# A part of the value product and the sum over keys moved in among the score tiles, in three attention cores on one Trainium2 core

## The reference

```python
x = x + jnp.tanh(g_xattn[n]) * xattn_ref(_layernorm(x), ctx_512, ...)
x = x + jnp.tanh(g_ffn[n]) * ffn_ref(_layernorm(x), ...)
```

```python
scores = jnp.einsum('bhsr,bhlr->bhsl', q_r, k_r)      # 16 heads, 56 queries, 1500 keys
attn = jax.nn.softmax(scores, axis=-1)
ctx_c = jnp.einsum('bhsl,bld->bhsd', attn, kv_rope)    # 64 wide
```

## Time and profile before

| | us |
|---|---|
| median of 3 runs | 2179.44 (2172.59 to 2183.32) |
| profiled execution | 2182.55 |
| its span, first to last instruction | 2180.8 |
| PE busy | 2052.8 |
| DVE busy | 1477.5 |
| POOL busy | 1356.4 |
| ACT busy | 1082.2 |

### The profile page before, as it was taken

The page is one execution under the profiler, slowest core; times in us unless marked ns, Lnnn a source line. Parts: engine busy times, 40 slices in busy tenths (PEclk is TensorE's granted clock), DMA queues, the critical chain, the costliest instruction groups (busy, mean ns, idle before and its releaser), DMA issues.

```text
span 2180.8 us, 34757 instructions
## 1 busy us (share of the span) xinstructions
PE 2052.8 (94%) x13336; PEld 1413.8 (65%) x13336; DVE 1477.5 (68%) x2141; ACT 1082.2 (50%) x1770; POOL 1356.4 (62%) x850
## 2 busy tenths in 40 slices
PE   7898999999999988899999999989998999999998
PEld 5586777755555556666555555488897555555588
DVE  6766872577887856766787887653335778878553
ACT  4452332565665645311566566444434656656543
POOL 0366883188788774455678778725441887887644
PEclk9898999999999998999999999999999999999999
DMA  3035877323223204101322322025533232232012
GB/s 97 3 118 162 249 230 211 93 57 80 63 57 81 48 30 129 34 1 35 84 57 65 78 58 66 7 87 156 146 95 76 58 80 63 58 80 49 32 46 76
DMA packets 65702, 179.56 MB, mean 82 GB/s; under 512 B 11280, under 2 KB 21280, under 8 KB 65154
## 3 DMA queue, kind: packets, MB, share of 16 engines
q1 hardware_dynamic: 65154, 177.01, 30.7%
q10 hardware_dynamic: 384, 0.33, 0.1%
HBM read 162.32 MB, written 14.98 MB: 81 GB/s over the span
## 4 chain that ended last, share of the span: by engine, by line
PE 76%; DVE 9%; ACT 4%; POOL 4%; issue 4%; DMA 1%; SPq 1%; POOLq 0%; DVEq 0%; ACTq 0%
PE psum L1529 19%; PE psum L946 19%; PE psum L1515 18%; PE psum L1405 5%; PE psum L1416 3%; ACT E L1984 3%; PE psum L1687 2%; PE psum L1546 2%; PE psum L1644 1%; DVE mx L2531 1%; PE psum L960 1%; POOL CL L2003 1%; PE psum L1339 1%; PE psum L1217 1%; PE psum L1237 1%
## 5 line engine op out<-in xcount | busy, mean ns | idle before, releaser
L2264 POOL TENSOR_TENSOR SA<-SA,E 125x896 f32<-125x896 f32 x288 | 605.9, 2104 | 19.1
L2531 DVE TENSOR_REDUCE mx<-psum 128x2 f32<-128x1000 f32 (+1 forms) x540 | 548.7, 1065 | 97.5 <-PE psum L1405 61.6
L1984 ACT ACTIVATE E<-psum 125x896 f32<-125x896 f32 x576 | 519.2, 920 | 128.4 <-PE psum L1515 101.2
L1529 PE MATMUL psum<-E,V 125*64 125x448 f32 x2304 | 459.5, 541 | 0.0
L1529 PEld LDWEIGHTS psum<-E,V 125*64 125x64 f32 x2304 | 159.9, 137 | 239.9 <-issue 228.1
L1515 PE MATMUL psum<-QH,KH 64*125 64x448 f32 x1152 | 256.1, 410 | 9.7 <-ACT E L1984 3.6
L2553 DVE RECIPROCAL RS<-psum 128x448 f32<-128x448 f32 x48 | 142.0, 2958 | 150.5 <-PE psum L1546 150.5
L1515 PE MATMUL psum<-QL,KH 64*125 64x448 f32 x1152 | 238.2, 363 | 0.0
L1515 PE MATMUL psum<-QH,KL 64*125 64x448 f32 x1152 | 222.4, 363 | 0.0
L1405 PE MATMUL psum<-KH,QH 64*128 64x500 f32 x864 | 194.9, 409 | 1.8 <-ACT QR L1926 1.6
L2264 POOL TENSOR_TENSOR SA<-SA,SB 125x896 f32<-125x896 f32 x45 | 105.7, 2348 | 132.8 <-DVE SB L2549 132.5
(11 more groups left out here) (310 smaller groups left out, 4179.5 us busy)
## 6 DMA issues: line engine op xcount, KB each, us to landing
KH<-kt_scratch SPq DMA_DIRECT2D x96, 375.0 KB, 5.2
KL<-kt_scratch SPq DMA_DIRECT2D x96, 375.0 KB, 6.8
EW<-in_f_w SPq DMA_DIRECT2D x64, 256.0 KB, 7.3
kt_scratch<-kt SPq DMA_DIRECT2D x16, 750.0 KB, 6.1
WS<-in_f_w SPq DMA_DIRECT2D x31, 384.0 KB, 4.9
GB<-gates_scratch SPq DMA_DIRECT2D x36, 224.0 KB, 3.9
slot_of_t<-slots_scratch SPq DMA_DIRECT2D x64, 112.0 KB, 3.8
WoT<-in_a_WoT SPq DMA_DIRECT2D x24, 256.0 KB, 3.4
```

The costliest lines, as they stand in the source:

```text
L1529: i = e.matmul(psum[c * DC:(c + 1) * DC, 4, 0:HT], V[0:LP, b, tile * DC:(tile + 1) * DC], E[g[n, b, k] % NE][0:LP, half[c]], start=k == 0, ...
L1984: e.activation(E[m % NE][0:LP, :].rearrange("p (c q) -> p c q", c=2), psum[0:LP, pair:pair + 2, 0:HT], ACT.Exp).then_inc(exp_set.sem, 1)
L2264: e.tensor_tensor(SA[b % 2][0:LP, :], a[0:LP, :], x[0:LP, :], ALU.add).then_inc(sum_set.sem, 1)
L2531: e.tensor_reduce(o, psum[:, max_banks(kind, *t), 0:CW], AX.X, ALU.max).then_inc(small_free.sem, 1)
```

## The change

Four things. `STEPS_AT` shifts the maxima of b + 1 among the score tiles. Behind tile k = 7 now stand `high` and `diag` of b + 2, `total` of b - 1, and the values of tiles 0 to 3; behind the twelfth tile follow `add` at once and the values of tiles 4 to 11, with `max_spread` behind values 6. `total` writes bank 5 instead of bank 0, so `low_end` 0 of the next maxima waits for its reciprocal, and `total` waits for the reduce of `max` (1, 2) in the same bank. Two waits ahead of head 0 go.

```diff
-STEPS_AT = {0: (0,), 1: (1,), 2: (2,), 3: (3,), 4: (4,), 6: (5,), 7: (6,), 8: (7,), 9: (8,), 10: (9,), 11: (10, 11)}
+STEPS_AT = {0: (0,), 1: (1,), 2: (2,), 3: (3,), 4: (4,), 5: (5,), 7: (6,), 8: (7,), 9: (8, 9), 10: (10,), 11: (11,)}
+WEAVE_AT, WOVEN = 7, 4
@@ core_order
             if k == 4 and b + 1 < B:
                 order.append(("low", b + 1))
+            if k == WEAVE_AT:
+                order += [("high", b + 2), ("diag", b + 2)] if b + 2 < B else []
+                order += [("total", b - 1)] if b > 0 else []
+                order += [("values", b, v) for v in range(WOVEN)]
         order.append(("again", b))
         order += [("max_total", b + 1)] if b + 1 < B else []
-        for k in range(NL):
+        order.append(("add", b))
+        for k in range(WOVEN, NL):
             order.append(("values", b, k))
-            if k == 1 and b + 2 < B:
-                order += [("high", b + 2), ("diag", b + 2)]
-            if k == 2:
-                order += [("total", b - 1)] if b > 0 else []
-                order.append(("add", b))
-            if k == 7 and b + 1 < B:
+            if k == WOVEN + 2 and b + 1 < B:
                 order.append(("max_spread", b + 1))
@@ small_bank
         if kind == "total":
-            return 0 if b < B - 1 else 1
+            return 5 if b < B - 1 else 1
@@ pe_core, low_end
                 if c == 0:
                     e.wait_ge(*diag_set.at(n, b))
+                    if b >= 2:
+                        e.wait_ge(*small_free.at(n, "total", b - 2))
@@ pe_core, head
-                        if b > 0:
-                            e.wait_ge(*small_free.at(n, "max_end", b, 2))
-                        if b > 1:
-                            e.wait_ge(*small_free.at(n, "total", b - 2))
@@ pe_core, total
-                e.wait_ge(*exp_set.at(n, min(b + 1, B - 1), NL - 2))
+                if b == B - 1:
+                    e.wait_ge(*exp_set.at(n, b, NL - 2))
+                elif b + 2 < B:
+                    e.wait_ge(*small_free.at(n, "max", b + 2, 1, 2))
```

## The result

| | before | after |
|---|---|---|
| median, us | 2178.49 of 4 runs (2172.59 to 2183.32) | 2197.51 of 4 runs (2195.09 to 2201.30) |
| profiled execution, us | 2182.55 | 2196.99 |
| its span, us | 2180.8 | 2195.2 |

The ratio is 1.009, with an interval of 1.0061 to 1.0119: the change costs 19 us, where 18 were forecast (2197.4). That is under 1% of the time, but clear of the spread of the runs.

What follows compares the result with a forecast made beforehand. PE, busy 94% of the span, was taken as the bound. 14 batches at +0.45 us, +0.35 for the first and -0.65 for the last give +6.0 a layer, +18.0 for three: 2179.4 to 2197.4 us, range 2181 to 2209.

Steps and rivals of the forecast that it cites:

- first batch of a layer: Batch 0 of each changed layer, where no total is woven: +0.35 us, against +0.45 for each of 14 other batches.
- The turnaround: Tiles 8 to 11: DVE's and ACT's waits start anew at low_end 0, so stalls return and the stretch takes 5.04 us.
- The reciprocal: Between weave and tile 8: low_end 0 waits for DVE's reciprocal of the total until 12.31, 0.13 us beyond PE's own pace.
- max (1, 2) at k = 5: Tiles 0 to 7: this maximum, moved from k = 6, waits for a DVE reduce: +0.1 us a batch (0 to 0.2).
- The turns: PE's two extra switches between score and value form around the weave: 0.21 us in all, range 0 to 0.3.
- modelled tails: At the two switches of array form: if each cost the last matmul's full tail, 0.36 and 0.54 us, the sum is about +25.
- The last batch: End of each changed layer: adds no longer wait for batch 14's reciprocal, so adds and total come 0.65 us earlier.
- A: Rival: the weave pays, tiles 8 to 11 run without the DVE stall, values at 16.2; -33 us, 2146; chance 0.10.
- B: Rival: a wash; max (1, 2) is free, head 11 doesn't wait, switches vanish in the reciprocal's wait; +5 us, 2184; chance 0.14.
- C: Rival: dearer switches of array form, entry +0.07 and exit +0.10 us, 8 us on top, 2205; chance 0.12.

## Why the prediction was right

Its own list of what the changed profile would show, in offsets from a batch's first maximum, in us. Measured is the batch that starts at 499.44.

| step | predicted | measured |
|---|---|---|
| last score pair of tile 7 | 8.00 | 7.95 |
| first pass of the total | 8.29 | 8.24 |
| reciprocal starts, ends | 9.30, 12.26 | 9.26, 12.22 |
| low_end 0 | 12.31 | 12.37 |
| low_end 1 | 14.10 | 14.14 |
| max (2, 2) | 15.21 | 15.25 |
| head 11 | 16.38 | 16.40 |
| values 4 | 17.39, taken as 17.35 | 17.42 |
| tiles 8 to 11 | 5.04 | 5.05 |
| batch | 23.75 (+0.45) | 23.80 (+0.50) |
| first batch of a layer | +0.35 | +0.31 |
| last batch of a layer | -0.65 | -0.63 |
| a layer | +6.0 | +6.7 |

**The turnaround.** That the stalls of tiles 8 to 11 hang on DVE and ACT and not on the time since the batch began was the step on which all rested, and it holds in the batch itself (5.05 us twice), in the value tile put ahead of low_end 2 or one tile earlier (2171 and 2182 us), and in the order that starts DVE earlier (2165).

So the account of a batch has two parts. The gain that the weave was to bring is nothing, as the stalls come back. The price is 0.50 us: 0.09 for the turn in and 0.05 for max (1, 2), which are the 0.14 ahead of the weave; 0.14 that the woven passes take more there than in the values phase, most of it the turn back; and 0.22 of waiting for the reciprocal.

**The reciprocal.** Its wait was put at 0.13 us a batch and was 0.22, by the copy in its place. The term too small is the way from DVE's end to PE's start: 0.05 was put, as it is behind a reduce (0.73 from its start to the matmul, of which the reduce takes 0.68), and 0.15 was measured (511.66 to 511.81; 0.14 with the total alone). Why it is longer behind the reciprocal no run separates. Half of it was made up by luck, by max (1, 2) at k = 5, which cost 0.05 instead of 0.1: low_end 0 came at 12.37 for 12.31. The total with nothing woven behind it shows that the reciprocal and not the value tiles sets low_end 0.

**The turns.** From scores to values 0.29 us where a pair follows after 0.20, and 0.12 back, both as taken from the earlier trace rows. From the last woven value pass to low_end 0 PE alone needs 3.11 us for sixteen passes (512.01 to 515.12, with the copy), which is the same as in the earlier trace rows. The Trainium skill's page "TensorEngine Tiling (Array Packing)", Key Properties, has a change of tiling mode drain the array. The kernel changes it twice in this place, and the rows show 0.09 and 0.12 us for it, less than the modelled tails of 0.36 and 0.54 us by which the sum would have been +25; measured was +19. What part of the 0.09 and 0.12 is a drain no run here separates.

**The last batch.** It runs from 785.25 to 805.73 until its total, 20.48 us for 21.11 before (782.07 to 803.18):

```profile
805.73 0.97 PE L1548 MATMUL psum<-SA,ones 125*64 125x448 f32 x4 [1.41 <-DVE SB L2551]
```

PE still waits for DVE's adds there, 1.41 us for the 1.89 of the earlier trace rows. The adds start 16.97 us into the batch for 17.63 before, as they no longer stand behind the reciprocal of batch 14, and wait for the later `again` instead:

```profile
802.22 2.23 DVE L2548 TENSOR_TENSOR psum<-psum,E 125x896 f32<-125x896 f32 x2 [5.32 <-ACT psum L1969]
```

**The rivals.** A (2146) is out: the values start at 17.42, not 16.2, and they do so at 16.95 even with reduces of a quarter's length. B (2184) had head 11 not wait; it waits for exp 9 in after, with the copy, with short reduces and with six tiles woven, and where the maxima stand in their old places head 10 and low_end 2 wait instead. C (2205) needed turns of 0.07 and 0.10 more than taken, and they have their rows' length. C lies only 0.17 us a batch, 8 us in all, from the forecast, so it is the rows at the turns that put it out and not the total. The sum of the table, 14 x 0.50 + 0.31 - 0.63 = 6.7 us a layer, is 20 for three, beside 19 in the medians.

**What went wrong** lies in the expectations of the experiments. Where a wait is removed or filled, I took the whole of it as gain (8 and 9 us came of some 20, with the value tile in the stall and with low_end 2 behind the head), but a filling that is longer than the hole pushes what follows. Where a cover was shortened (six woven tiles), I looked at the stretch that was edited and not at the chain that had been hidden by it and ends in the next batch.

## What to carry to other kernels

A stall behind another engine's turnaround moves with the matmul that feeds that engine: work put ahead of that matmul fills nothing, and only what stands between feeder and waiter does, and that no further than its own length and turns fit. Before filling such a stall, try to start the feeder earlier; here half a maximum put ahead of one head gained 0.7% (13 us in the medians), where the weave ahead of the same stretch lost 19 us. And work that is moved away from a place also covered something there: list what ends late in it, into the next iteration too.

## What the runs showed of the hardware

**An idle wait of PE cost twice.** In the kernel with the total alone PE waits 3.15 us for the reciprocal in each batch. Two stretches of it, up to and through the wait and behind it, with the granted clock in the third column from the end:

```profile
508.00:520.00 12.00, 9.09 (x74) 6.08 (x74) 10.79 (x8) 8.78 (x12) 8.44 (x5) 1.00 0.00 0
520.20:526.30 6.10, 6.06 (x29) 5.30 (x31) 3.76 (x4) 1.97 (x3) 5.94 (x4) 0.50 0.00 0
```

Behind the wait the granted clock is 0.50, the 1.2 GHz level, and here it is back at 1.00 some 6.5 us on. This is a long one: in layer 2 two of the fourteen stretches are of this length, the others 3 to 4 us (the expectation of the kernel with PE kept at work took the 6 us for each batch). The thirteen batches between its first and fourteenth division are 27.59 to 28.75 us long (27.88 on average); with PE kept busy by matmuls of no use, and at a clock of 1.00, they are 26.95. That is 0.93 us a batch, 39 for 42 of them. The executions are 33 us apart, since the added matmuls are not hidden in the last batches and cost some 10 us there; the few us that this leaves over lie between the cores, within the spread of single runs.

The last batches of the kernel with six tiles woven show it with a shorter wait: behind 2.9 us without a matmul the granted clock of the next stretch was 0.57 and 0.76 in layers 3 and 4, and 1.00 in layer 2. Behind the 1.41 and 1.89 us of after and before it is 1.00 in all three layers.

In after the four value tiles fill the wait for the reciprocal, and the granted clock is 1.00 in all four stretches of the batch. To take them out again and leave the total where it is does not save, but lose: 2366 us for 2198.
